# A graph layer on one core: SyncE fetches two of the 202 pairs row by row, ScalarE issues the feature transfers

## The reference

```
h   = relu(layernorm(x))
W   = silu(edge_attr @ fw1 + fb1) @ fw2 + fb2          # one row of 128 per edge
y   = silu(h @ aw1 + ab1) @ aw2 + ab2                  # one row of 128 per node
agg = segment_sum(W * y[src], dst, 6250)               # rows of y fetched by edge
out = silu(agg @ ow1 + ob1) @ ow2 + ob2
result = x + h + out
```

## Time and profile before

| | us |
|---|---|
| three runs | 2031.39, 2034.52, 2033.88 |
| median | 2033.88 |
| profiled execution | 2030.81 |
| its span | 2028.9 |
| busy: POOL / PE / DVE / ACT | 1522.7 / 1214.7 / 1194.5 / 297.2 |
| granted TensorE clock, mean | 0.769 |

### The profile page before, as it was taken

How to read it: one execution, slowest core, us unless ns; L and a number is a source line. 1 busy time by engine, 2 the same in 40 slices (tenths; PEclk the granted TensorE clock), 3 DMA queues, 4 the chain that set the end, 5 groups by cost and what they waited for, 6 DMA issues and landing times.

```text
span 2028.9 us, 15293 instructions
## 1 busy us (share of the span) xinstructions
PE 1214.7 (60%) x5635; PEld 915.1 (45%) x5735; DVE 1194.5 (59%) x1505; ACT 297.2 (15%) x343; POOL 1522.7 (75%) x1619
## 2 busy tenths in 40 slices
PE   5555665655666557656666565565555555556555
PEld 3344444544454445445444454444444444444444
DVE  7675555655565556556655565556555555555555
ACT  5311111111111111111111111111111111111110
POOL 7777777777777777777777777777777777777775
PEclk9777777887777777877777778778777777777766
DMA  6432231332332232222332322232232331331221
GB/s 194 160 95 89 58 95 53 94 100 52 95 100 57 95 94 79 74 94 53 100 93 53 95 94 68 84 98 84 67 99 53 97 95 53 99 95 52 67 54 50
DMA packets 62301, 171.62 MB, mean 85 GB/s; under 512 B 27088, under 2 KB 29648, under 8 KB 59024
## 3 DMA queue, kind: packets, MB, share of 16 engines
q0 software_dynamic: 51584, 105.75, 19.5%
q1 hardware_dynamic: 8192, 61.32, 8.0%
q10 hardware_dynamic: 2448, 3.54, 0.5%
HBM read 164.08 MB, written 6.42 MB: 84 GB/s over the span
## 4 chain that ended last, share of the span: by engine, by line
POOL 72%; issue 24%; DMA 1%; DVE 1%; PE 1%; ACT 0%; POOLq 0%; SPq 0%; ACTq 0%; DVEq 0%
POOL xg L393 72%; DMA node_table<-res 1%; DVE res L595 0%; DMA rows<-in_rows 0%; DVE stats L581 0%; PE banks L828 0%; DVE sums L691 0%; PE banks L822 0%; ACT hs L425 0%; DMA xg<-node_table,src 0%; DVE hT L547 0%; PE banks L833 0%; DVE xs L553 0%; DVE banks L695 0%; DVE banks L688 0%
## 5 line engine op out<-in xcount | busy, mean ns | idle before, releaser
L393 POOL DMA_INDIRECT xg<-node_table,src x1564 | 1475.9, 944 | 477.5 <-issue 476.3
L688 DVE TENSOR_TENSOR banks<-banks,xg 128x1024 f32<-128x1024 f32 (+1 forms) x198 | 241.2, 1218 | 777.3 <-DMA xg<-node_table,src 751.0
L898 PEld LDWEIGHTS banks<-wts,hid 128*128 128x128 f32 x3224 | 633.8, 291 | 60.0 <-issue 37.9
L898 PE MATMUL banks<-wts,hid 128*128 128x128 f32 x3224 | 622.4, 375 | 3.5 <-DVE sums L691 3.5
L894 PE MATMUL banks<-fb_rows,ones_b 128*128 128x512 bf16 x303 | 149.2, 558 | 674.3 <-DVE sums L691 671.9
L691 DVE TENSOR_REDUCE sums<-banks 128x128 f32<-128x1024 f32 (+1 forms) x408 | 494.0, 1211 | 13.7
L456 ACT ACTIVATE hid<-banks,cols 128x1024 f32<-128x1024 f32 x202 | 224.5, 1111 | 1630.1 <-PE banks L886 1630.1
L894 PEld LDWEIGHTS banks<-fb_rows,ones_b 128*128 128x128 bf16 x403 | 28.9, 110 | 710.4 <-DVE sums L691 688.3
L886 PE MATMUL banks<-attr,wts 50*128 50x512 f32 x806 | 261.6, 729 | 1.5 <-ACT hid L456 1.3
L695 DVE TENSOR_TENSOR banks<-banks,other 128x1024 f32<-128x1024 f32 (+1 forms) x204 | 248.7, 1219 | 7.0
L906 PEld LDWEIGHTS banks<-onehot,sums 128*128 128x128 f32 x816 | 109.0, 194 | 148.5 <-issue 142.2
(11 more groups left out here) (88 smaller groups left out, 285.5 us busy)
## 6 DMA issues: line engine op xcount, KB each, us to landing
attr<-in_attr SPq DMA_DIRECT2D x25, 2048.0 KB, 8.1
xg<-node_table,src POOLq DMA_INDIRECT x1564, 2.5
out<-res ACTq DMA_DIRECT2D x8, 256.0 KB, 2.3
xs<-in_x SPq DMA_DIRECT2D x3, 512.0 KB, 7.5
node_table<-res SPq DMA_DIRECT2D x3, 512.0 KB, 3.5
out<-res ACTq DMA_DIRECT2D x5, 192.0 KB, 2.7
spare<-in_dst SPq DMA_DIRECT2D x1, 808.0 KB, 11.0
src<-in_src SPq DMA_DIRECT2D x1, 808.0 KB, 13.5
```

The source lines that it names most:

```text
L393: pool.indirect_dma_start(xg[:, i % XG, j, :], None, table[:, :], bass.IndirectOffsetOnAxis(ap=src[:, s * L + j:s * L + j + 1], axis=0))\
L688: dve.tensor_tensor(to, to, rows_of, ALU.mult).then_inc(signal, 1)
L898: i = pe.matmul(to[:, at], hid[:, s % 2, at], w["fw2_s"][:, :], start=False, stop=j % TPG == TPG - 1)
```

## The change

`ROW_TURNS = (100, 196)` names two pairs that leave `MAIN_TURNS`. SP fetches their 2 x 1024 rows into a buffer of their own, `row_x`. It waits until the table is complete, then goes through the edges in order of tile and partition: for sixteen edges one load of sixteen indices from device memory into registers, then sixteen transfers of one row of 512 bytes to one partition, each with its source address computed from a register. Each of the eight tiles of a pair has a semaphore in `row_in`. In turns 100 and 196 DVE reads `row_x` and waits for the eight semaphores at 16 x 128 each. POOL has no gather there.

The feature transfers move from SP to ACT (`features`), and `PART` goes from 8 to 4, so they are 1 MB each. The first two are issued before ACT clears `agg`, the transfer for turns s+4 to s+7 in turn s, behind the activation of turn s+2. A host-side array `row_src` holds the two pairs' indices in the order of the fetch.

```diff
-PART = 8
+PART = 4
+ROW_TURNS = (100, 196)
+ROWS_AT_ONCE = 16
+ROW_OF = {s: m for m, s in enumerate(ROW_TURNS)}
-MAIN_TURNS = [s for s in range(PAIRS) if s not in EARLY_TURNS]
+MAIN_TURNS = [s for s in range(PAIRS) if s not in EARLY_TURNS and s not in ROW_TURNS]
...
+        row_x = sb("row_x", [P, len(ROW_TURNS), L, F])
...
+        row_in = [[sem(f"row_in{m}_{j}") for j in range(L)] for m in range(len(ROW_TURNS))]
...
-            def pair(s):
-                if s % PART == 0:
-                    n = min(PART, PAIRS - s)
-                    if s >= 2 * PART:
-
-                        sp.wait_ge(pe_turn, run(s - PART - 1))
-                    at = s % (2 * PART) * GC
-                    sp.dma_start(attr[:, at:at + n * GC], attr_t[:, s * GC:(s + n) * GC]).then_inc(attr_in[s // PART % 2], 16)
-
-            for s in range(PAIRS):
-                pair(s)
+            sp.wait_ge(s_tab, 16 * (AHEAD + table_writes(N_CHUNKS - 1)))
+            for m in range(len(ROW_TURNS)):
+                for a in range(0, PAIR_EDGES, ROWS_AT_ONCE):
+                    j, p = divmod(a, P)
+                    _, rows_of = nc.values_load_multi_w_load_instructions(
+                        row_src_t[m:m + 1, a:a + ROWS_AT_ONCE], engines=[sp.engine], min_val=0, max_val=NODE_TILES * P - 1)
+                    for i, row in enumerate(rows_of):
+                        sp.dma_start(row_x[p + i:p + i + 1, m, j, :], table[bass.ds(row, 1), :]).then_inc(row_in[m][j], 16)
...
+            def features(s):
+                n = min(PART, PAIRS - s)
+                if s >= 2 * PART:
+                    act.wait_ge(pe_turn, run(s - PART - 1))
+                at = s % (2 * PART) * GC
+                act.dma_start(attr[:, at:at + n * GC], attr_t[:, s * GC:(s + n) * GC]).then_inc(attr_in[s // PART % 2], 16)
...
+            features(0)
+            features(PART)
...
+                if s % PART == 0 and PART <= s < PAIRS - PART:
+                    features(s + PART)
...
+                elif s in ROW_OF:
+                    rows_of = row_x[:, ROW_OF[s], :, :]
+                    for landed in row_in[ROW_OF[s]]:
+                        dve.wait_ge(landed, 16 * P)
```

More of the change, by code:

```diff
@@ L185, in after, with gnn_layer @@
     return run(s + FILL)
-def gnn_layer(nc, x, e_src_t, src_t, dst_t, attr_t, node_wts_t, wts_t, cols_t, rows_t, out):
+def gnn_layer(nc, x, e_src_t, src_t, row_src_t, dst_t, attr_t, node_wts_t, wts_t, cols_t, rows_t, out):
     f32, i32, bf16 = mybir.dt.float32, mybir.dt.int32, mybir.dt.bfloat16
@@ L1018 @@
         "src": np.ascontiguousarray(src_p.transpose(1, 0, 2).reshape(P, EDGE_TILES)),
+        "row_src": np.ascontiguousarray(src_p[list(ROW_TURNS)].transpose(0, 2, 1).reshape(len(ROW_TURNS), PAIR_EDGES)),
         "dst": np.ascontiguousarray(dst_p.transpose(1, 0, 2).reshape(P, EDGE_TILES)),
```

## The result

The changed kernel takes 2019.12 us in the median of four runs (2018.09 to 2020.14), the kernel before 2034.2 in four (2031.39 to 2035.03). The ratio is 0.9928 with a 95% interval of 0.9911 to 0.9945: 15 us faster, where 20 were forecast. The profiled execution took 2018.09 us, its span is 2016.3.

A forecast was written before the change was run, and what follows sets the result against it. POOL's list of gathers was taken to bound the kernel: the 2033.88 us median less 20.0 us for sixteen gathers, other changes costing nothing, gave 2013.9 us. Its own range was 2009 to 2018, the outer range 2009 to 2200.

The forecast's parts named there:

- Bound by POOL, 1.248 us a gather, 20.0 us for sixteen: POOL's gather list sets the span; removing sixteen gathers at 1.248 us each should bring 20.0 us to the end.
- SP is in time: SP's row fetch at 14.3 us per sixteen rows completes the pairs 50 and 63 us ahead of need.
- Loads with the add: On SP, two register loads and a small add per sixteen rows: 1.1 us, upper end 8.5 us.
- Checks: On SP, sixteen bound checks of two instructions each: 0.31 us apiece, 5.0 us per group, 10% either way.
- Address and transfer together: On SP, sixteen address computations at 0.18 us (2.9 us) and sixteen one-row transfers at 0.33 us (5.3 us).
- The formula, last row + 41: If the second pair's last row lands late at T2, remaining turns and tail make the span T2 + 41 us.
- The break-even at 0.939 us a row: SP's time per row at which the whole 20 us gain is given back; full gain below 0.929.
- A turn's gap of 5.5 us: DVE reaches the turn after a row-fed turn's predecessor 5.5 us later, where POOL's pace was 10 us.
- "Cost 0" for the features: ACT issuing 51 feature transfers of 1 MB, 24 us in all, lies in idle time and adds 0 us.
- The rival on loads by the register: SP's load of sixteen costs per register: loads and add 3.1 us, 1.02 us a row, run some 2198 us; chance 0.20.
- Row transfers disturbing POOL: Rival: SP's row transfers share DMA engines and make gathers 1% later, 1.261 us, about 2034 us; chance 0.04.
- features late in the turns: Rival: feature transfers come late behind ACT's work, PE waits every fourth turn, 2064 us; chance 0.02.

The follow-up runs named there:

- the collision at the start removed: Changed kernel with ACT's first two feature transfers issued only after the table is complete: 2011.15 us, ratio 0.9906 to the kernel before.
- three pairs, with SP's list made shorter: Changed kernel with turns 68, 132, 196 by rows, no bound checks, late first features, index list in SBUF: 2001.27 us, ratio 0.9857.
- The two late kernels: Changed kernel with three pairs by rows, late first features, no bound checks: 2024.13 us; changed kernel with eight indices per register load: 2122.81 us.
- the last profile: The changed kernel run again without edit on a fourth chip, where the kernel before took 2030.31 us: 2016.01 us, ratio 0.9929.

## Why the prediction was right, and where not

- **Bound by POOL, 1.248 us a gather, 20.0 us for sixteen: right.** With the collision at the start removed the change brings 19.5 us, and three pairs, with SP's list made shorter, 29.0 of 30.
- **SP is in time: right, with 100 us to spare where 63 were expected, but by luck.** The group was forecast at 14.3 us and measured at 14.06, by errors that cancel. Loads with the add: 1.1 forecast, 1.09 + 1.73 + 0.05 and gaps, some 3.0, measured. The only row for a load was of one register from SBUF (`n_left`), and the list lies in device memory. Checks: 5.0 forecast, 147 + 18 ns and gaps, about 0.25 each or 4.0, measured. Address and transfer together: 2.9 + 5.3 = 8.2 forecast, 16 x 0.42 = 6.7 measured. These make 13.7; most of the rest are loads slower than the median, up to 3.9 us. A transfer of one row costs SP 225 ns, not 290 as taken without its gap, and two multiplications 37 ns, not 140; a MOVE of 29 ns, which the order doesn't show, comes on top.
- **The formula, last row + 41: right to 1.5 us.** The two late kernels gave + 42.4 and + 41.9 from the last row's issue, though I had no late kernel to read it from. The 1.4 us from its issue to the multiplication were left out. The break-even at 0.939 us a row follows from it and was not run by itself. A turn's gap of 5.5 us after an unhindered turn was 5.6.
- **"Cost 0" for the features: the step that failed.** I priced the transfers in the turns, each against its use, and those are free. The first two I never placed in time. The order showed them ahead of the clearing of `agg`; in the trace of before that clearing began at 56.57 us, when the last table writes, which everything waits for, were on their way. Before, SP issued those writes ahead of the features on its own queue, and even the last write, in flight while features were issued, took 3.04 us. Now the last write but one took 8.80. Measured: 2.5 us in the first profile, 4.5 us alone (ratio 1.0022), 4.9 us in the last profile against the second of the kernel before.
- **The size:** 2019.12 against 2013.9, 1 us above the forecast's own range of 2009 to 2018. 15 of 20 us came. The outer range, up to 2200, covers most of the rivals too, so that the time lies in it says little for the forecast.
- **The rival on loads by the register was half right.** They do cost by the register, but at 0.106 us each, a fifth of what its upper end took. Loads and add passed the 1.8 us from which it was to decide, and it did not decide only because cheaper checks and transfers paid for it. The rule of the Trainium skill ("Runtime: NRT & Kernel Launch", "Instruction fetch mechanics") that a load costs by the register agrees with the trace in kind, eight and sixteen being 0.89 and 1.73 us; its 200 ns is about twice what they show.
- **Row transfers disturbing POOL, features late in the turns:** neither came about. The gathers kept to 1.2486 us beside the rows, and PE's list of waits has no line for features.

## What to carry to other kernels

Work taken from the engine that bounds comes back in full only if the helper is on time, so compare its pace with the deadline of each piece, not its total with the span; beyond the deadline every microsecond counts. When a transfer is moved to another queue, look where its first instance starts: an order that one queue gave for free is gone. A helper made of thousands of short instructions needs a wide margin: the five per cent of this one were gone where instructions came slower, as on one chip here.

## What the runs showed of the hardware

- Addressed by a register, one row of 512 bytes costs SP 225 ns for the transfer and 0.42 us from one to the next with its address step. Transfers of 128 partitions took 328 ns, and 0.475 us when two followed straight on each other.
- A load of registers from device memory: 0.89 us for eight, 1.73 us for sixteen, 0.106 us for each register more. From SBUF it is 1.26 us for sixteen and 0.47 for one. The load of a two-register address from device memory took 1.09 us, which this line doesn't fit; all but the first stood right behind a transfer, and whether that is why is open.
- A table write of 192 KB landed after 3.0 to 3.4 us without feature reads beside it and after 8.7 to 9.4 us beside 2 MB of them from ACT's queue. How the DMA engines divide their time between two queues is not shown by this.
- One gather of the changed kernel took 944 ns in the profile of the last chip and 947 in that of the first comparison, with the same program: 4 us in 2000 between executions that nothing in the program explains.
- On one chip all kernels were slowed, by 19% for the kernel before and by 61% for the changed one, with single instructions 1.4 us apart.
